# Another order of work within a tile, an own start sequence for four tiles, and x loaded batch by batch

## What is computed

```
mod = silu(c) @ wmod                       # six rows of 256 per batch: sa, ca, ga, sb, cb, gb
h   = layernorm(x) * (1 + ca) + sa
q, k, v = split(h @ qkv_w + qkv_b)         # 16 heads of 16
local  = softmax(mask(q k^T / 4)) v        # window of 128 keys before the query
pooled = mean of h over chunks of 16 tokens
lat    = softmax(mask(rq rk^T / 4)) rv     # rq from h, rk and rv from pooled, 4 heads of 16
remote = lat @ rout_w + rout_b
gate   = sigmoid(local @ gl_w + remote @ gr_w)
x1     = x + ga * ((gate * local + (1 - gate) * remote) @ out_w + out_b)
h2     = layernorm(x1) * (1 + cb) + sb
out    = x1 + gb * (layernorm(h2 + routed) * ln_g + ln_b)   # routed: attention among 64 tokens picked per head
```

## Time and profile before

| | us |
|---|---|
| median of three runs | 733.73 (728.38 to 739.91) |
| the profiled execution's own time | 729.22 |
| its span, first to last instruction | 727.2 |

### The profile page before, as it was taken

One profiled execution on the slowest core, in us unless ns is written; L12 is line 12 of the kernel. 1 busy time (PEld: TensorE's weight loads), 2 busy tenths in 40 slices (PEclk: granted clock), 3 DMA queues, 4 the chain that ended last, 5 costly groups with the idle time before them and its releaser, 6 DMA issues. The chain is left out here.

```text
span 727.2 us, 21665 instructions
## 1 busy us (share of the span) xinstructions
PE 532.0 (73%) x7351; PEld 397.0 (55%) x7351; DVE 444.5 (61%) x1268; ACT 363.3 (50%) x897; POOL 384.8 (53%) x552
## 2 busy tenths in 40 slices
PE   2650478788887787788887787888877778888862
PEld 2330355666665556566665556666656556666641
DVE  5351177757665577666654577676655776666654
ACT  1211156656555556665654465565555565665550
POOL 3221065656555556556554556565654566565563
PEclk9955599999999999999998999999998999999996
DMA  7249434434435081706053443444260717071430
GB/s 230 79 177 235 67 67 73 66 69 74 75 60 90 24 119 36 110 31 118 31 88 41 72 76 74 74 70 79 54 95 25 113 35 117 31 111 38 82 45 22
DMA packets 98207, 57.72 MB, mean 79 GB/s; under 512 B 9108, under 2 KB 96300, under 8 KB 98092
## 3 DMA queue, kind: packets, MB, share of 16 engines
q1 hardware_dynamic: 95228, 54.94, 40.3%
q10 hardware_dynamic: 2864, 1.31, 0.7%
HBM read 38.64 MB, written 17.59 MB: 77 GB/s over the span
## 5 line engine op out<-in xcount | busy, mean ns | idle before, releaser
L1170 DVE TENSOR_REDUCE mtok<-p_x 128x3 bf16<-128x480 f32 (+3 forms) x192 | 113.4, 591 | 108.9 <-issue 55.7
L593 ACT ACTIVATE pr<-p_y 128x512 f32<-128x512 f32 x232 | 132.2, 604 | 32.8 <-PE p_y L809 32.8
L455 POOL TENSOR_TENSOR rstd<-ve,half 128x1 f32<-128x1 f32 x106 | 64.1, 605 | 106.8 <-DVE ve L1091 106.4
L808 PE MATMUL p_y<-qst,kst 112*128 112x128 bf16 x464 | 72.4, 223 | 48.9 <-ACT pr L593 46.9
L730 PE MATMUL p_qkv<-hT,wqk 128*128 128x256 f32 x280 | 92.1, 487 | 1.0 <-ACT hT L562 0.9
L445 POOL TENSOR_SCALAR_AFFINE_SELECT pr<-pr 128x512 f32<-128x512 f32 x132 | 87.5, 664 | 3.7 <-ACT pr L593 3.7
L809 PE MATMUL p_y<-qst,kst 112*128 112x128 bf16 x528 | 79.0, 221 | 6.0 <-ACT pr L595 6.0
L430 POOL TENSOR_TENSOR qkf<-qkf,terms 128x512 f32<-128x512 f32 x34 | 39.3, 1155 | 82.5 <-ACT terms L572 82.5
L449 POOL TENSOR_SCALAR_AFFINE_SELECT pr<-pr 128x512 f32<-128x512 f32 x116 | 81.3, 700 | 0.0
L808 PEld LDWEIGHTS p_y<-qst,kst 112*128 112x128 bf16 x464 | 43.4, 98 | 64.7 <-issue 51.5
L730 PEld LDWEIGHTS p_qkv<-hT,wqk 128*128 128x128 f32 x280 | 63.6, 238 | 13.3 <-ACT hT L562 1.3
(11 more groups left out here) (146 smaller groups left out, 1156.6 us busy)
## 6 DMA issues: line engine op xcount, KB each, us to landing
qst<-scr_q SPq DMA_DIRECT2D x102, 128.0 KB, 4.9
kst<-scr_k SPq DMA_DIRECT2D x102, 128.0 KB, 4.3
scr_q<-terms SPq DMA_DIRECT2D x17, 384.0 KB, 2.9
scr_k<-terms SPq DMA_DIRECT2D x17, 384.0 KB, 2.8
out_y<-y SPq DMA_DIRECT2D x32, 128.0 KB, 1.7
x_all<-in_x SPq DMA_DIRECT2D x1, 3072.0 KB, 17.3
pr<-in_wmod SPq DMA_DIRECT2D x1, 1024.0 KB, 10.1
x_all<-in_x SPq DMA_DIRECT2D x1, 768.0 KB, 5.0
```

Source lines behind the costliest of these rows:

```text
L455: pool.tensor_tensor(rstd_[:, :], ve_[:, :], half[:, :], ALU.pow).then_inc(s_rstd, 1)
L593: act.activation(pr[:, 2 * i:2 * i + 2, :, :], src, ACT.Exp).then_inc(exp_done[i], 1)
L808: pe.matmul(p_y[i % 2][:, at:at + P], kst[0:KS + H, h, (n - 1) % NB, :], q, start=True, stop=True)
L1170: dve.tensor_reduce(mtok[:, KS + h0:KS + h1], p_x[i % 2][:, 0:(h1 - h0) * w].rearrange("p (h n) -> p h n", n=w), AX_X, ALU.max, negate=Tru ...
```

## The change

Nothing is computed otherwise; the same instructions are issued in another order.

- In each engine's `slot` the order is new. Pairs are taken odd first (scores 1, 0, 3, 2, 5, 4; scores_t and exps likewise, except that ACT takes exps 2 before 3). The gate chain comes earlier: `out_tokens` after the first transposed pair, `local_out` ahead of `scale2` and `shift2`, `difference` ahead of the masks, `gate_tanh` after exps 3. On PE all four `sum_v` stand at the end, in the order 1, then `project_out`, then 3, 2, 0; `scores(t, 4)` moves behind the last transposed pair. On ACT `part1` and `part2` stand before `shift`, on POOL `res1` and `part3` at the start.
- DVE's list before: `bn1(a) bn2(d) moments1(a) pool_tokens(k) moments2(d) add_eps1(a) maxima(t,0) add_eps2(d) lat_max(t) maxima(t,1) copy_v(k) maxima(t,2) maxima(t,3) norm1(a) prob_sum(c) maxima(t,4) prob_recip(c) maxima(t,5) scale2(d) shift2(d) local_out(c) copy_rv(k) copy_rk(k) gate_dif(c) bn3(d) lat_recip(t) mix_heads(c) copy_rq(k) moments3(d) lat_norm(t) add_eps3(d) scale3(d) copy_qk(h) finish(d) spread_rv(k) first_residual(c)`
- DVE's list after: `bn1(a) pool_tokens(k) bn2(d) moments1(a) add_eps1(a) maxima(t,1) lat_max(t) maxima(t,0) norm1(a) maxima(t,3) copy_v(k) prob_sum(c) moments2(d) prob_recip(c) add_eps2(d) local_out(c) lat_recip(t) scale2(d) maxima(t,5) maxima(t,2) shift2(d) lat_norm(t) bn3(d) copy_rq(k) moments3(d) copy_rk(k) gate_dif(c) copy_rv(k) add_eps3(d) mix_heads(c) scale3(d) spread_rv(k) copy_qk(h) maxima(t,4) finish(d) first_residual(c)`
- The start of tiles 0 to 3 is a sequence of its own on each engine. On DVE the modulation rows are made before the weights; its list is bn1, moments1, add_eps1 (0), bn1 (1), norm1 (0), moments1, add_eps1, norm1 (1), copy_qk (0), bn1, moments1, add_eps1 (2), copy_qk (1), norm1 (2), modulation_rows, bn1, moments1, add_eps1 (3), weights, norm1 (3), pool_tokens, copy_v, copy_rv, copy_rk, copy_rq, spread_rv (0), copy_qk (2), two scale_wo. The waits for the scaled output weights stand in `project_out`, not ahead of the loop.
- On SP the first two `store_terms` and `load_stack` come before the modulation rows; x of batches 1, 2 and 3 (1 MB each) is loaded after slots 0, 2 and 4 of the first batch. The buffers of the modulation rows lie in x's place for batches 2 and 3.

```
+
+LAST_ST, LAST_PV, LAST_MAX = 6, 0, 4
 EPS = 1e-5
...
 
-SU_SILU, SU_MODT, SU_PRE = 3, 16, 29
-SU_ROWS = SU_PRE + 13
-SU_ALL = SU_ROWS + B // 2 + 1
+SU_SILU, SU_MODT, SU_ROWS = 3, 17, 30
+SU_PRE = SU_ROWS + 13
...
 
 
-        mrow6 = pr[0:B, 4:12, :, :].rearrange("p h a n -> p (h a n)").rearrange("p (j d) -> p j d", d=D)
-        ga = pr[:, 0:4, :, :].rearrange("p h a n -> p (h a n)")
...
             sp.dma_start(x_all[:, (XPAD + 2) * D:(XPAD + NB) * D].rearrange("p (t d) -> p t d", d=D),
                          x[2:NB].rearrange("t p d -> p t d")).then_inc(loaded_x1, 16)
 
-            sp.wait_ge(su_dve, SU_ROWS)
-            sp.dma_start(mod_rows.rearrange("j b d -> b j d"), mrow6[:, 0:6, :]).then_inc(rows_stored, 16)
-            sp.wait_ge(rows_stored, 16)
-            sp.dma_start(ga, mod_rows[0].rearrange("b d -> (b d)").partition_broadcast(P)).then_inc(loaded_g, 16)
-            for j, tile in enumerate((obg, s1, c1, g3, b3)):
...
+                sp.wait_ge(rows_stored, 16)
+                sp.dma_start(ga, mod_rows[0].rearrange("b d -> (b d)").partition_broadcast(P)).then_inc(loaded_g, 16)
+                for j, tile in enumerate((obg, s1, c1, g3, b3)):
+                    sp.dma_start(tile[:, D:], mod_rows[1 + j].rearrange("b d -> (b d)").partition_broadcast(P))\
+                      .then_inc(loaded_t, 16)
+
+            def load_batch(b):
+
+                if b > 1:
...
 
                 half = r[1] % 2
...
                 if Q and t[1] % 2 == 0:
                     load_stack(r)
 
-            slot((0, -2), "Q")
-            slot((0, -1), "Q")
+            for r in ((0, 0), (0, 1)):
+                store_terms(r)
+                load_stack(r)
+            store_rows()
             for n in range(NB):
                 slot((0, n), "Q" if n < 3 else "QD")
+                if n in (0, 2, 4):
+                    load_batch(n // 2 + 1)
+            sp.wait_ge(loaded_x, 16 * B)
...
 
 
...
                 if t[1] == 0:
-
+                    wait_apart(pool, (x1_ready, done(back(t, 1))), (loaded_x, t[0] * 2 + 16))
                     pool.wait_ge(loaded_t, 16 * 5)
-                    pool.wait_ge(loaded_x, 16)
+                else:
+                    wait_apart(pool, (x1_ready, done(back(t, 1))))
...
-                if D:
-                    add_u(d)
+                if Q:
+                    res1(r)
                 if A:
                     rstd1(a)
                 if Q:
-                    res1(r)
+                    part3(r)
                 if D:
-                    rstd2_of(d)
-                if Q:
-                    part3(r)
-                if T:
-                    mask(m, 0)
+                    add_u(d)
                 if C:
                     add_bias(c)
                     difference(c)
-                if T:
+                if D:
+                    rstd2_of(d)
+                if T:
+                    mask(m, 0)
                     mask(m, 1)
+                    mask(m, 2)
                 if D:
                     rstd3_of(d)
                 if T:
-                    mask(m, 2)
                     mask(m, 3)
...
-            slot((0, -4), "A")
+            b0, b1, b2, b3_ = (0, 0), (0, 1), (0, 2), (0, 3)
+            rstd1(b0)
+            rstd1(b1)
             scale_weights()
-            slot((0, -3), "AP")
-            slot((0, -2), "APQ")
-            slot((0, -1), "APQK")
+            res1(b0)
+            rstd1(b2)
+            part3(b0)
+            res1(b1)
+            part3(b1)
+            rstd1(b3_)
             pool.wait_ge(loaded_g, 16)
             for b in range(B // 2):
                 scale_wo(pool, b, su_pool)
-
-            pool.wait_ge(su_pool, SP_ALL)
-            pool.wait_ge(su_dve, SU_ALL)
-            pool.wait_ge(loaded_x1, 16)
...
+                if Q:
+                    part1(r)
                 if C:
                     out_t(c)
-                if T:
-                    shift(m)
-                if Q:
-                    part1(r)
-                if T:
-                    lat_oT(m)
-                    exps(m, 0)
                 if Q:
                     part2(r)
                 if T:
-                    exps(m, 1)
+                    shift(m)
+                    lat_oT(m)
                 if S:
                     lat_exp(t)
                 if T:
+                    exps(m, 1)
+                    exps(m, 0)
+                if A:
+                    modulated(a)
+                if T:
                     exps(m, 2)
                     exps(m, 3)
-                if A:
-                    modulated(a)
-                if T:
-                    exps(m, 4)
                 if C:
                     gate_tanh(c)
                 if T:
+                    remote(m)
                     exps(m, 5)
-                    remote(m)
+                    exps(m, 4)
+                    exps(m, 7)
                     exps(m, 6)
-                    exps(m, 7)
+                if C:
+                    mixed_t(c)
                 if S:
                     lat_pT(t)
-                if C:
...
-            slot((0, -4), "A")
-            slot((0, -3), "AP")
-            slot((0, -2), "APQ")
-            slot((0, -1), "APQK")
-            act.wait_ge(su_dve, SU_ALL)
-            act.wait_ge(su_pool, SP_ALL)
+            b0, b1, b2, b3_ = (0, 0), (0, 1), (0, 2), (0, 3)
+            modulated(b0)
+            modulated(b1)
+            part1(b0)
+            part2(b0)
+            modulated(b2)
+            part1(b1)
+            part2(b1)
+            modulated(b3_)
             run(act, slot)
...
-                if i == 0 and t[1] % 2 == 0:
+                if i < 2 and t[1] % 2 == 0:
...
-                pe.wait_ge(s_max[NS - 2], done(t))
-                pe.wait_ge(s_max[NS - 1], done(t))
+                pe.wait_ge(s_max[LAST_MAX], done(t))
...
-                if g == 0:
-
-                    pe.wait_ge(oT_ready, done(back(t, 1)))
+                pe.wait_ge(oT_ready, done(back(t, 1)))
...
-                pe.wait_ge(mixT_ready, done(t))
+                pe.wait_ge(su_dve, SU_ALL)
+                pe.wait_ge(su_pool, SP_ALL)
...
                 if T:
                     max_t(m)
                 if S:
+                    scores(t, 1)
                     scores(t, 0)
                     lat_scores(t)
                 if T:
                     lat_out_t(m)
                 if S:
-                    scores(t, 1)
+                    scores(t, 3)
                 if K:
                     project_v(k)
+                if T:
+                    scores_t(m, 1)
+                if C:
+                    out_tokens(c)
                 if T:
                     scores_t(m, 0)
                 if S:
                     scores(t, 2)
-                if T:
-                    scores_t(m, 1)
-                if C:
-                    out_tokens(c)
-                if S:
-                    scores(t, 3)
-                if T:
-                    lat_remote(m)
-                    scores_t(m, 2)
-                    scores_t(m, 3)
-                if S:
-                    scores(t, 4)
                 if A:
                     ln_t(a)
                 if T:
-                    sum_v(m, 0)
+                    lat_remote(m)
                 if S:
                     scores(t, 5)
                 if T:
-                    scores_t(m, 4)
-                    scores_t(m, 5)
+                    scores_t(m, 3)
+                    scores_t(m, 2)
                 if K:
                     project_lat(k)
                 if T:
-                    scores_t(m, 6)
-                if T:
-                    scores_t(m, 7)
+                    scores_t(m, 5)
+                    scores_t(m, 4)
                 if PR:
                     project_half(h)
+                if T:
+                    scores_t(m, 7)
+                    scores_t(m, 6)
+                if S:
+                    lat_p_t(t)
+                    scores(t, 4)
                 if C:
                     mixed_t(c)
-                if S:
-                    lat_p_t(t)
+                if T:
+                    sum_v(m, 1)
                 if C:
                     project_out(c)
                 if T:
-                    sum_v(m, 1)
+                    sum_v(m, 3)
                     sum_v(m, 2)
-                    sum_v(m, 3)
-
+                    sum_v(m, 0)
...
-            slot((0, -4), "A")
+            b0, b1, b2, b3_ = (0, 0), (0, 1), (0, 2), (0, 3)
+            ln_t(b0)
             pe.wait_ge(su_act, SA_QK)
-            slot((0, -3), "AP")
+            ln_t(b1)
+            project_half(b0)
+            project_half(b1)
+            ln_t(b2)
             pe.wait_ge(loaded_m2, 16)
             modulation_rows()
-            slot((0, -2), "APQ")
+            ln_t(b3_)
             pe.wait_ge(su_dve, SU_PRE)
+            project_v(b0)
             pe.wait_ge(su_pool, SP_SCALED)
-            slot((0, -1), "APQK")
```

(36 more changed lines are left out.)

118 lines of the change are left out of this document (58 added, 60 removed).

## The result

| | us |
|---|---|
| before, median of 4 runs | 736.82 (728.38 to 740.13) |
| after, median of 4 runs | 622.30 (619.26 to 623.93) |
| ratio | 0.8508, 95% interval 0.8423 to 0.8592 |
| the profiled execution of after, its span | 623.93, 621.9 |

The change is faster by 15%.

The account below looks back on a forecast made before the run. A chain of waits through all four engines, none full, bounds the loop; the start waits for the k stack. Span 57 + 18 + (4 x 128 - 16) + 11 + 3 + 27.5 = 612.5, giving 618 us, range 598 to 680.

Parts of the forecast that it names:

- its own signs: Signs of being right: first scores before 60 us without k stack wait, slots 16 to 16.5, tanh not waiting for difference.
- its signs of being wrong: PE gaps above 1 us outside project_v's front, PEclk near 0.91 in most slots, or even slots' scores awaiting the k stack.
- The start: Before the loop: the 26.5 us k stack wait goes, first slot opens at 57 (52 to 62), slot 0 takes 18.
- The gate chain: Middle of a slot: local_out ends by +6.5, difference by +7.3, tanh finds its input ready, the 1.64 us gap goes.
- A slot's length: Loop slots: 14.6 work, 1.3 front gap, 0.25 before project_out make 16.2 us against 18.21; slots n = 1 take 14.8.
- The k stack in even slots: Slot 1's k stack is due 13.6 us into a slot of 14.8: 2.5 to the store, 11.0 from store to scores.
- The clock: PE's stretches at 1.2 GHz: none inside slots, one of 1.5 us after each turn of the loop.
- The x loads: Three 1 MB loads on SP in the first batch: 3 us for slot 1, nothing for the two others; ends 0 and 12.
- The turn: Each of three loop turns costs 2.1 us net wait plus 1.5 of clock, 3.6; 11 in all, ends 6 and 16.
- The drain: After the loop: only the first of three slots changes, 2 us off 29.5, leaving 27.5; ends 0 and 4.
- the copies of the start: In the start, two projections of 3.78 us and their copies, in a row, end at 31.5 us.
- new wait: Rival: the order brings a wait of about the old size, say DVE; slots stay near 18.2, 678 us; chance 0.14.

Follow-up runs that it names:

- e_noq: The changed kernel without the stores and loads of the q stack after the first pair of tiles (output no longer the block's); 592.4 us.
- e_q_gate: e_q_x with GpSimd's difference moved back behind masks 0 and 1, and the second rstd ahead of them; 714.6 us.
- e_q_x: e_qfirst with the three 1024 KB loads of x at the end of slots 1, 3 and 5 of the first batch instead of 0, 2 and 4; 603.0 us.
- e_qfirst: The changed kernel with SP's q stack loads ahead of the store of y in even slots; 606.8 us, or 607.6 without one slow execution.
- e_best2: e_best1 with all four batches in one pass of the loop, so no turn is left inside the work; 568.1 us.
- e_q_turn: e_qfirst with two batches in a pass of the loop on PE, ScalarE, VectorE and GpSimd, leaving one of three turns; 599.2 us.
- e_start: The changed kernel with every engine's slot except SP's in the order of before, keeping the changed start; 704.9 us.
- e_slots: The kernel before with the changed order in the loop's slots alone, its start and x load as before; 635.1 us.
- e_best1: e_q_x plus e_q_turn's loop, modulation rows stored ahead of the first k loads, and part2 behind the shift in even slots alone; 580.0 us.

## Why the prediction was right

The time was forecast as 618 and is 622.3; of the span, 612.5 was forecast and 621.9 came. That it came so near is luck, since large errors cancelled:

| term, us | forecast | measured |
|---|---|---|
| opening of the first slot | 57 | 53.67 |
| slot 0 | 18 | 21.48 |
| slots 1 to 31, no waits at openings | 496 | 475.5 |
| waits at even openings (the x loads among them) | 3 | 28.9 |
| turns | 11 | 12.0 |
| drain | 27.5 | 31.3 |

475.5 is four times the last batch of e_noq, 123.08, less its slot 0, 16.81. These rows make 622.9, 1 us more than the span; they leave out what the clock loses behind the waits and count a wait in full though it covers its slot's front gap, which go opposite ways. By its own signs the prediction was right on the first scores and on tanh; slots were shorter than it said, and two of its signs of being wrong came: waits above 1 us at other places of PE, and scores waiting at the opening of even slots.

- **The start: right.** The first scores ran at 53.87, and no wait for the stack stood there. The terms in it were off both ways. PE opened 3.3 us sooner. Slot 0 was 3.5 longer, since its first maxima stood behind VectorE's scaling of weights, and that behind the gate rows: "its part1 starts only after the last copy" named a smaller cause. These are the rows:

```profile
53.97 2.37 DVE L288 TENSOR_TENSOR wo<-rem,x_all 128x512 f32<-128x512 f32 x2 [0.36 <-DMA x_all<-mod_rows]
```

```profile
58.27 0.50 PE L789 MATMUL p_x<-smask,ident_bf 128*128 128x384 bf16 x1 [2.85 <-DVE mtok L1192]
```

- **The gate chain: right.** Tanh found its input ready, as forecast. local_out started at 110.97 in the slot opened at 105.35, +5.6, where "by +6.5" was said for its end. e_q_gate shows that the slots' gain hangs on it: with the difference late, 112 us go.
- **A slot's length: the terms "14.6 + 1.3 + 0.25" were too large.** Undisturbed slots take 15.3 to 15.4. PE's busy time is 14.0 to 14.6 in them; the gap in front of project_v, in e_q_x, is 1.26 in n = 3 as forecast, 1.00 in n = 2, and 1.06 to 0.81 in n = 4 to 7, where the prediction said "nearer to 1.0"; and the 0.25 ahead of project_out is gone altogether. Slots n = 1 take 13.9, where 14.8 was said.

```profile
236.86 1.16 PE L757 MATMUL p_qkv<-wv,hT 128*128 128x272 f32 x4 [1.26 <-issue]
...
267.62 1.16 PE L757 MATMUL p_qkv<-wv,hT 128*128 128x272 f32 x4 [0.83 <-issue]
```

- **The k stack in even slots: the step that failed.** It said "In slot 1 the k stack is due 2.5 + 11.0 = 13.6 into a slot of 14.8" (the sum is 13.5), and nothing of the later slots. The slot n = 1 of the second batch, opened at 211.85, shows which of these numbers failed:

```profile
211.08 2.79 SPq L382 DMA_DIRECT2D qst<-scr_q  x6
214.39 0.38 SPq L367 DMA_DIRECT2D scr_k<-terms  x1
221.12 2.76 SPq L382 DMA_DIRECT2D kst<-scr_k  x6
...
228.92 0.35 PE L797 MATMUL p_x<-edge,ident_bf 128*32 128x192 bf16 x4 [2.98 <-issue]
```

  The 2.5 holds. The slot takes 13.9, and from store to scores it is 14.5 instead of 11.0, 17.1 in all, so that PE stands 2.98. The 11.0 came from one pair of rows whose store had a clear queue, 6.5 us into its slot. A store at 2.5 stands right behind the q loads, and the round trip became 13.2 to 14.5 in the slots n = 1, 3 and 5 of this batch (in 3 and 5 the q loads hold up the store's issue as well, to 3.8 and 3.4). e_qfirst and e_noq show that the q loads are the cause. That the wait was listed among the signs that would prove it wrong is what made it quick to find.
- **The clock: "I take none in the slots" failed with it.** The granted clock fell in the third slots, behind waits of 3 us (228.92 in the slot of 0.83). Without these waits it doesn't: the slots of e_q_x shown have 1.00. The Trainium skill ("TensorE: Matmul & The Clock Gate", section "A second HAM failure mode: psum-queue depth-cycling") tells of a kernel in which frequent short idles between groups of matmuls made the clock swing. Gaps of the size here didn't: e_best2 has gaps of up to 1.27 from slot to slot, none longer, and 1.00 over 480 us.
- **The x loads: near for slot 1, wrong for the others.** For slot 1, 3 us were charged, and PE waited 1.64 at the next opening. "nothing for the two others, whose slots are longer": there it waited 2.31 and 5.84 (at 158.85, behind the last load).
- **The turn: right in size.** PE waited 3.67, 3.47 and 4.89; the 3.6 forecast for each was a net price, with 1.2 off for work that runs meanwhile and 1.5 on for the clock. e_q_turn gives 3.8 for a turn as a whole.
- **The drain: "I take 2 off" had the wrong sign.** It grew by 1.9 us (31.34 against 29.49), with 4.71 us of waiting for mix where it was 4.15. It is the slots' order that does it: e_start, with the old slots, has a drain of 29.7, e_slots, with the old start, one of 31.6. Which step of the order isn't shown; in e_q_gate the wait for mix is 4.08, but another of 3.2 comes in, and its drain is 33.6.

Of the smaller sums, the copies of the start make 31.3, not 31.5. No rival came true whole. The "new wait" did come, at about half of the size given for it (28.9 of 60 us), and for a DMA instead of an engine.

## What to carry to other kernels

When a slot shrinks, or a store in it moves up, a transfer that stood alone in its queue can come to stand right behind others, and its round trip gets longer: work out anew which transfers stand ahead of the one that is due, in each kind of slot. Large loads belong ahead of a store that is due late (x ahead of the q store here), and a load shouldn't stand in the queue's program behind a store that waits for output, if a store that is due early comes next. And in a loop with strict orders on each engine a single step at a wrong place (here one difference of 1 us) can hold back the others, so follow the chain that sets the pace first.

## What the runs showed of the hardware that wasn't expected

The length of a gap alone doesn't fix what the clock does: in e_q_gate project_half took 1.97 us behind a wait of 2.68, and 3.61 behind one of 2.62 in the next slot.

From the issue of a store of 384 KB to that of the loads that wait for it, 2.8 to 3.3 us passed in nearly all slots where the queue was free (before, and e_noq), 4.9 to 6.8 where six loads of 128 KB had been issued just ahead (after; 9.6 once, with 1024 KB of x just ahead as well), and 3.2 to 4.8 in e_qfirst from the second batch on, where the q loads had been issued earlier and only the y store since.

PE paused at times in the middle of a row of equal matmuls. e_best1 has 4.0 us of this in six places, e_best2, which has no turn, 1.0 us in two. It isn't the loop as such: the changed kernel has one such pause and e_noq none, both with three turns. The longest in e_best1, in the summing of values, came with five of 48 matmuls still to do. The last row is from the DMA view of 234.7 to 236.4 us:

```profile
235.27 1.49 PE L845 MATMUL p_pv<-pr,vp 128*18 128x128 f32 x43
237.79 0.40 PE L845 MATMUL p_pv<-pr,vp 128*18 128x128 f32 x5 [1.03 <-issue]
...
q8 instruction: 1, 0.02, 5.8%
```

That row is one transfer of instructions, of 16 KB; 5.8% of the time of 16 engines over 1.7 us make 1.6 us for it. All 45 such pauses in the traces, in nine kernels, end 1.2 to 1.7 us after the end of a transfer of this kind that had taken 1.6 to 1.8 us, where the shortest take 0.9; most of the slow ones bring no pause. So PE seems to have waited for its own instructions. No run tried it, and what makes the transfers slow is open.

The pauses (3.0 us less), the one turn (3.28) and an opening of the first slot 1.6 us sooner explain 7.9 of the 11.9 us between e_best1 and e_best2; the rest is open. Longer code cost nothing that these runs show.
